# A sparse-mask residual and an attention block on one core: another order of tile projections, row maxima and head outputs around the pairs

## The reference

```python
# step 1: the 10240 largest entries of a scaled outer product get +1 (diagonal excluded)
adj = s * cond * softmax(x) / sqrt(n)            # 1024 x 1024 a batch
x = x + (1.0 at the top_k(adj, 10240), else 0.0)
# step 2: conditioned RMS norm, attention with 16 heads of 64, output projection
xn = rms_norm(x, g_norm) * (1 + scale) + shift   # scale, shift = cond @ W_emb + b_emb
q, k, v = split(xn @ W_qkv); q = rms_norm(q, g_q); k = rms_norm(k, g_k)
o = softmax(q @ k.T / 8) @ v
x = x + o + o @ W_out
```

## Time and profile before

| what | value |
|---|---|
| median of 3 runs | 3984.5 us (3980.17 to 3985.11) |
| the profiled execution, its own time | 3988.51 us |
| its span in the trace | 3986.8 us |
| mean granted TensorE clock | 0.978 |
| busy: PE, DVE, ACT, POOL | 3743.1, 2619.9, 1537.1, 1260.9 us |

### The profile page before, as it was taken

How to read it: one execution, slowest core, us unless ns; L and a number is a source line. 1 busy time by engine, 2 the same in 40 slices (tenths; PEclk the granted TensorE clock), 3 DMA queues, 4 the chain that set the end, 5 groups by cost and what they waited for, 6 DMA issues and landing times.

```text
span 3986.8 us, 44387 instructions
## 1 busy us (share of the span) xinstructions
PE 3743.1 (94%) x16035; PEld 2436.3 (61%) x16035; DVE 2619.9 (66%) x4521; ACT 1537.1 (39%) x2724; POOL 1260.9 (32%) x1880
## 2 busy tenths in 40 slices
PE   5885899999998999999998999999998999999999
PEld 2333676666644766667644667667644667666644
DVE  8996677777787677777787677777787333233321
ACT  1004344444434344444434344444433244444430
POOL 2005433333315433333315433333314433333300
PEclk9997799999999999999999999999999999999999
DMA  4003000001025100000125100000033100000022
GB/s 159 0 5 116 17 22 22 22 22 37 22 91 192 34 22 22 22 22 22 33 96 184 42 22 22 22 22 22 22 107 132 47 22 22 22 22 22 22 81 88
DMA packets 165296, 193.68 MB, mean 49 GB/s; under 512 B 7336, under 2 KB 120032, under 8 KB 164064
## 3 DMA queue, kind: packets, MB, share of 16 engines
q1 hardware_dynamic: 165088, 190.98, 15.0%
HBM read 142.72 MB, written 48.23 MB: 48 GB/s over the span
## 4 chain that ended last, share of the span: by engine, by line
PE 73%; DVE 15%; ACT 4%; POOL 4%; issue 3%; DMA 1%; SPq 0%; DVEq 0%; ACTq 0%; POOLq 0%
PE pax L1209 23%; PE ppv L1278 19%; PE pst L1265 10%; PE pax L1245 7%; PE pst L1190 7%; DVE trash L797 3%; DVE xr L832 3%; DVE mx L985 3%; PE pax L1227 2%; POOL xn L419 2%; PE ppv L1209 2%; PE pax L1253 1%; ACT sA L666 1%; DMA pt<-out_x 1%; PE pst L1083 1%
## 5 line engine op out<-in xcount | busy, mean ns | idle before, releaser
L1209 PE MATMUL pax<-wh,xn 128*128 128x384 f32 x3840 | 1060.5, 347 | 21.9 <-POOL xn L419 21.9
L1278 PE MATMUL ppv<-pt,v 128*65 128x512 f32 x2048 | 990.9, 595 | 1.1 <-issue 1.1
L797 DVE TENSOR_SCALAR_CACHE_REDUCE trash<-keys,state 128x2048 uint8<-128x2048 f32 x384 | 900.1, 2344 | 9.8
L985 DVE TENSOR_REDUCE mx<-pax 128x1 f32<-128x512 f32 x960 | 618.6, 686 | 227.5 <-PE pax L1245 207.0
L1209 PEld LDWEIGHTS pax<-wh,xn 128*128 128x128 f32 x3840 | 704.9, 189 | 35.7 <-issue 35.7
L673 ACT ACTIVATE pt<-pst 128x1024 f32<-128x1024 f32 x512 | 524.0, 1023 | 506.2 <-PE pst L1265 447.9
L1209 PE MATMUL pax<-wl,xn 128*128 128x384 f32 x1920 | 649.1, 338 | 0.0
L971 DVE TENSOR_REDUCE ss<-sq 128x4 f32<-128x256 f32 x256 | 107.2, 419 | 759.8 <-ACT sq L648 759.8
L1245 PE MATMUL pax<-sA 65*128 65x512 f32 x960 | 466.0, 531 | 21.9 <-ACT sA L661 13.0
L1278 PEld LDWEIGHTS ppv<-pt,v 128*65 128x65 f32 x2048 | 278.8, 137 | 298.3 <-issue 224.6
L395 POOL TENSOR_TENSOR wl<-wf,wh 128x1024 fp32r<-128x1024 f32 x96 | 228.7, 2387 | 579.0 <-ACT wh L544 579.0
(11 more groups left out here) (144 smaller groups left out, 4574.6 us busy)
## 6 DMA issues: line engine op xcount, KB each, us to landing
wf<-in_L_cond_W_qkv SPq DMA_DIRECT2D x96, 512.0 KB, 5.4
keys<-in_x SPq DMA_DIRECT2D x32, 512.0 KB, 9.8
xin<-in_x SPq DMA_DIRECT2D x32, 512.0 KB, 4.0
out_x<-xin SPq DMA_DIRECT2D x32, 512.0 KB, 3.2
wo<-in_L_cond_W_out SPq DMA_DIRECT2D x4, 4096.0 KB, 13.5
pt<-out_x SPq DMA_DIRECT2D x64, 256.0 KB, 4.0
out_x<-pt SPq DMA_DIRECT2D x64, 256.0 KB, 2.1
oT_scr<-ostg SPq DMA_DIRECT2D x56, 256.0 KB, 2.0
```

Source lines behind the costliest of these rows:

```text
L797: e.tensor_scalar(trash[:], kv, thr_f, None, ALU.is_ge, ALU.add, accum_out=cnt[:, c:c + 1]).then_inc(z_cnt, 1)
L985: e.tensor_reduce(mx2[:, j // T, j % T, c:c + 1], max_banks(alone, j)[:, c, :], axis=AX, op=ALU.max).then_inc(m_mx, 1)
L1209: i = e.matmul(qkv_bank(alone, t)[:, 0:6 * DH], xn[:, a, k, t * P:(t + 1) * P], w[:, k, :, :].rearrange("p s c -> p (s c)"), start=(k == 0 ...
L1278: i = e.matmul(ppv[0:DH + 1, c, :], v2[:, par, kt, hh, :], pt[:, kt % 2, c * HALF:(c + 1) * HALF], start=(kt == 0), stop=(kt == T - 1))
```

## The change

- **Two units ahead.** `scores` and `exp` of unit t + 2 now stand in unit t, so two score tiles are under way. Tile 0 is projected before unit 0, in two parts of 12 products, tiles 1 and 2 in unit 0, and tile t + 2 in units 1 to 5. `transpose_tile(t + 1)` stands right behind `prep_tile(t + 2)`. DVE's `prep_split` of a tile now stands in the tile's own iteration, between its two counts.
- **Maxima over more products.** The table `slots` gives for each of units 8 to 15 what stands between the two products of `values`, and twice what stands behind the scores. Before, one item stood in each of 18 gaps of units 9 to 15.
- **Both heads turned at the next pair's start.** `out_move` of head 0 goes to `ostg` and that of head 1 to `heads_t`; both `out_tokens` and `normalise` stand at the beginning of the next pair, or of the boundary. `max_row` of head 1 goes through `pst`.
- **Boundary.** SP stores a half before it waits to load the next tile. `add_half` comes earlier among the `finalise_tile`s, `prep_sums(gp, 0)` stands before the last `finalise_tile`, and PE projects one more half ahead of the features and of tile 0 (q = 3 to 7, then 8 with the features, then 9; before, q = 3 to 6, 7 with the features, then 8).
- POOL's `zero_row` waits for the previous pair's last values, not for tile 0.

```diff
+    def row_banks(hh):
+        return pst[:, 2:4, :] if hh else pax
+    def evicted(hh):
+        return heads_t if hh else ostg
...
-                    self.finalise_tile(fb, t)
+                    self.keep_tile(fb, t)
                 if ob is not None:
-                    if t == 1:
-                        self.store_half(ob, 0)
-                    if t > 0:
-                        self.store_half(ob, t)
+                    for q in ([0, 1], [2, 3], [4], [5], [6], [7], [8], [9])[t]:
+                        self.store_half(ob, q)
+                if fb is not None and t + 2 < T:
+                    self.next_tile(fb, t)
...
             if prep:
-                e.wait_ge(a_qkv, T * (gp + 1) + 1)
+                e.wait_ge(t_pv, CST + 2 * T * gp)
...
-        def out_move(self, gp, hh):
+        def out_move(self, gp, hh, stored):
             e, g = self.e, 2 * gp + hh
             e.wait_ge(t_pv, CST + T * (g + 1))
...
+            if hh == 0:
                 e.wait_ge(d_ost, 32 * stored + 16)
+            e.activation(evicted(hh)[0:DH + 1, :], ppv[0:DH + 1, :, :].rearrange("p a b -> p (a b)"),
+                         ACT.Copy).then_inc(t_mv, 1)
...
         def pair(self, b, i, par, search, prep, first):
             e, gp = self.e, PAIRS * b + i
+            z = STEPS * b + 4 * i
+            before = [step_before(b, i, t) if search else None for t in range(T)]
...
             self.exp(gp, 0, 0)
             self.max_row(gp, par, 1)
+            if prep:
+                self.prep_tile(gp + 1, 1 - par, 0, z=before[0])
+            elif search:
+                self.search_tot(before[0])
...
+            self.exp(gp, 0, 1)
+            if not first:
+                self.out_rows(gp - 1, 0)
+            for t in range(2 * T):
+                if t == T - 1:
+                    self.out_move(gp, 0, (PAIRS - 1) * b + i)
+                if prep and t == 0:
+                    self.prep_tile(gp + 1, 1 - par, 1)
+                if prep and t == 1:
+                    self.stack_tile(gp + 1, 1 - par, 1)
+                if prep and t == 12:
+                    self.max_row(gp + 1, 1 - par, 0)
+                if t + 2 < 2 * T:
+                    self.exp(gp, (t + 2) // T, (t + 2) % T)
                 if t == 0 and not first:
...
+                    self.out_rows(gp - 1, 1)
+                if prep and t == 0:
+                    self.stack_tile(gp + 1, 1 - par, 0)
+                    self.prep_tile(gp + 1, 1 - par, 2, z=before[2])
+                if prep and 1 <= t <= T - 3:
+                    self.prep_tile(gp + 1, 1 - par, t + 2, z=before[t + 2])
+                    self.stack_tile(gp + 1, 1 - par, t + 1)
+                if prep and t == T - 1:
+                    self.stack_tile(gp + 1, 1 - par, T - 1)
+                if prep and gp + 2 < PAIRS * B and t in (9, 11, 13):
+                    self.split_w(gp + 2, (t - 9) // 2)
...
             gp = PAIRS * fb
             self.ties(fb, 0)
-            self.ties(fb, 1)
             if ob is not None:
                 self.normalise(PAIRS * ob + PAIRS - 1, 1)
-            self.ties(fb, 2)
-            self.ties(fb, 3)
+            for c in range(1, 4):
+                self.ties(fb, c)
             self.ranks(fb)
             for t in range(T):
+                if t == T - 1 and ob is not None:
+                    self.prep_sums(gp, 0)
                 self.finalise_tile(fb, t)
                 if ob is None and t == 2:
                     self.conditioning()
-                if t == 1:
-                    self.add_half(ob, 0)
-                if t > 0:
-                    self.add_half(ob, t)
-            self.add_half(ob, 8)
-            self.prep_sums(gp, 0)
+                for q in ([0, 1], [2, 3], [4], [5], [6], [7], [8], [])[t]:
+                    self.add_half(ob, q)
+            if ob is None:
+                self.prep_sums(gp, 0)
             self.prep_split(gp, 0)
...
+            if not first:
+                for hh in range(2):
+                    self.normalise(gp - 1, hh)
             for t in range(T):
                 before = step_before(b, i, t) if search else None
                 if prep:
                     self.prep_sums(gp + 1, t)
-                    if t == T - 1:
-                        self.normalise(gp, 0)
-                    if t > 0:
-                        self.prep_split(gp + 1, t - 1)
-                    if before is not None:
-                        self.search_update(before)
-                    if search:
-                        self.search_count(z + t // 2, 2 * (t % 2))
-                    if t == T - 1:
-                        self.prep_split(gp + 1, t)
-                    if search:
-                        self.search_count(z + t // 2, 2 * (t % 2) + 1)
-                else:
-                    if t == T // 2:
-                        self.normalise(gp, 0)
-                    if before is not None:
-                        self.search_update(before)
-                    if search:
-                        self.search_count(z + t // 2, 2 * (t % 2))
-                        self.search_count(z + t // 2, 2 * (t % 2) + 1)
-            if search and not prep:
-                self.search_update(z + 3)
+                if before is not None:
+                    self.search_update(before)
+                if search:
+                    self.search_count(z + t // 2, 2 * (t % 2))
+                if prep:
+                    self.prep_split(gp + 1, t)
+                if search:
+                    self.search_count(z + t // 2, 2 * (t % 2) + 1)
             if prep:
                 for j in range(2 * T):
                     self.row_max(gp + 1, j)
-                self.normalise(gp, 1)
+            else:
+                self.normalise(gp, 0)
+                if search:
+                    self.search_update(z + 3)
...
+                if hh:
+                    e.wait_ge(t_mv, 2 * gp + 1)
+                else:
+                    e.wait_ge(t_on, CST + 2 * gp)
             e.wait_ge(t_ex, CST + w + 1)
...
             e, g = self.e, 2 * gp + hh
-            e.wait_ge(t_mv, g + 1)
+            e.wait_ge(t_mv, 2 * gp + 2)
+            e.wait_ge(t_on, CST + g)
...
         def pair(self, b, i, par, search, prep, first):
             e, gp = self.e, PAIRS * b + i
+            z = STEPS * b + 4 * i
+            before = [step_before(b, i, t) if search else None for t in range(T)]
...
+            slots = {8: [None, None, 0], 9: [1, 2, 3], 10: [4, 5, 6], 11: [7, None, None], 12: ["row", None, 8],
+                     13: [9, 10, 11], 14: [12, 13, 14], 15: [15, None, None]} if prep else {}
             if first and b > 0:
                 e.wait_ge(o_add, 2 * T * b - 2)
             self.scores(gp, par, 0, 0)
             if not first:
+                self.out_tokens(gp - 1, 0)
+            e.wait_ge(m_mx, 4 * T * (gp + 1))
+            if prep:
+                self.prep_tile(gp + 1, 0, hi=4)
+            if not first:
                 self.out_tokens(gp - 1, 1)
-            self.max_row(gp, 1)
+            e.wait_ge(t_ex, CST + 2 * T * gp)
             if first and b > 0:
                 e.wait_ge(o_add, 2 * T * b)
-            for t in range(T):
-                if t < T - 1:
-                    self.scores(gp, par, 0, t + 1)
-                else:
-                    self.scores(gp, par, 1, 0)
-                self.values(gp, par, 0, t)
-                if t == 0:
-                    e.wait_ge(m_ev, 2 * gp + 2)
-                    if not first:
-                        self.out_rows(gp - 1, 0)
-                if prep and t > 1:
-                    if t == 2 and not first:
-                        e.wait_ge(t_oe, 2 * gp)
-                    self.transpose_tile(gp + 1, t - 2)
-                if prep:
-                    self.prep_tile(gp + 1, t, z=step_before(b, i, t) if search else None)
-                elif search and t in (0, 4):
-                    self.search_sum(step_before(b, i, t // 2))
+            self.max_row(gp, 1)
+            if prep:
+                self.prep_tile(gp + 1, 0, z=before[0], lo=4)
+            elif search:
+                self.search_sum(before[0])
+            e.wait_ge(m_ev, 2 * gp + 2)
+            self.scores(gp, par, 0, 1)
+            if not first:
+                self.out_rows(gp - 1, 0)
+            for t in range(2 * T):
+                gap = slots.get(t, [None] * 3)
+                self.values(gp, par, t // T, t % T, lambda: fill(gap[0]))
+                if prep and t == 0:
+                    self.prep_tile(gp + 1, 1)
+                if prep and t == 1:
+                    self.transpose_tile(gp + 1, 1)
+                if t + 2 < 2 * T:
+                    self.scores(gp, par, (t + 2) // T, (t + 2) % T)
                 if t == 0 and not first:
                     self.out_rows(gp - 1, 1)
...
+                    e.wait_ge(t_oe, 2 * gp)
+                if prep and t == 0:
+                    self.transpose_tile(gp + 1, 0)
```

(33 more changed lines are left out.)

133 lines of the change are left out of this document (52 added, 81 removed).

## The result

| | median | runs | profiled span | granted clock |
|---|---|---|---|---|
| before | 3982.34 us | 4, 3978.39 to 3985.11 | 3986.8 us | 0.978 |
| after | 4078.23 us | 4, 4073.52 to 4078.43 | 4076.5 us | 0.977 |

What follows compares the result with a forecast made beforehand. PE was taken to bound the kernel, holding 73% of the chain that ended last. 3988.5 + 100 (pairs) - 14 (boundaries) + 1.5 (fourth last pair) = 4076 profiled, so 4072 us; range 3990 to 4112.

Steps and rivals of the forecast that it cites:

- Bunches: Units 9, 10, 13 and 14: two maxima in direct succession make PE stand 1.1 us each time, 4.4 us a pair.
- The second part: Pair from the first maximum on: contents, changes of kind, bunches and small waits sum to 30.7 us, 3.2 more than before.
- The first part: Pair up to the first maximum: loses 3.3 us, gains new waits, 67.9 us in all, bounds 66 and 69.5.
- tile 0's turning: At a pair's start, `transpose_tile(0)` waits 1.5 us for ACT's second `ostg` copy, which reads the bank it writes.
- two sums: Sums over partitions at even tiles' ends: PE waits 0.2 us for DVE two or three times, 0.5 us a pair.
- DVE's wait for POOL: In odd iterations of the first part, DVE's split waits for POOL's rounding: 1.0 us of idle.
- the rival of a slower POOL chain: POOL's chain, at 4.5 us, sets DVE's pace: 2.5 us more in 21 pairs with a search, 4125 us; chance 0.10.
- The pair: A pair of heads with preparation: 3.6 us more than 94.58, for 28 pairs +100 us.
- Last pair and boundary: Final sum 7 us later, boundary gains; net 4.7 us less each, three times -14; fourth last pair +1.5.
- the bunches cost little: Rival for maxima in succession: DVE is ready ahead of both products, so the kernel takes 3950 us, faster; chance 0.10.
- The boundary that gives more: Rival: DVE's boundary waits all go, each 15 us shorter, pairs cost only 1.5 more: 3982 us, no change; chance 0.07.
- the clock would not matter inside a pair: Granted clock stays 1.00 in a pair despite waits of 1 us; new waits at most 1.5 us, so nothing was priced.

Runs made afterwards that it cites:

- x1_spread: Changed kernel with the second of a unit's three maxima moved ahead of the unit's scores, unit 14's bunch kept: 4011.99 us, ratio 1.0059 to the kernel before.
- x4_before_bunched: Kernel before, with only four pairs of maxima put in direct succession in units 10 to 14: 4104.86 us, ratio 1.0297 to the kernel before.
- x2_rows_first: Changed kernel with `out_rows` and its `ostg` copy ahead of unit 2's scores and `exp`: 4065.46 us, ratio 1.0197 to the kernel before.
- x3_split_late: Changed kernel with DVE's splits of the odd tiles behind both counts of the iteration: 4074.72 us, ratio 1.0221 to the kernel before.
- x9_rows_and_split: Changed kernel with the `ostg` copy ahead of `exp` 2 and odd tiles' splits behind both counts, except tile 7's: 4032.57 us, ratio 1.0106 to the kernel before.
- x7_old_boundary: Changed kernel with the boundary's old order of stores, halves and `prep_sums` under the new pairs: 4103.02 us, ratio 1.0287 to the kernel before.
- x5_pax_row: Changed kernel; last pairs alone send the maxima row through `pax` between both `out_tokens`, sum and first `out_rows` behind unit 0's values: 4063.44 us, ratio 1.0186.

## Why the prediction was right

It gave 4072 us and the median is 4078.23. The main mechanism held. The closeness is in part luck: of the 4076 put for a profiled execution (4078.19 came), the pairs cost 25.5 us less than said and all that lies around them 27.7 more. The 4 us between the profiled execution and the median, which the kernel before had, are not there in the changed one.

- **Bunches.** 1.1 us of standing each, four a pair, was the largest term. By starts they are 1.09, 1.10, 1.10 and 1.09. The second part was put at 30.7 and takes 30.20; its single waits were put at 0.2 each and are 0.22 to 0.26. x1_spread takes 2.35 a pair away by order alone, and x4_before_bunched puts 2.9 into the kernel before by order alone.
- **The first part.** Put at 67.9, it takes 67.41. `out_tokens` waits some 0.3 (0.3 said), tile 0's turning 1.46 (1.5), two sums 0.17 and 0.16 (0.5), and unit 8 shows none. DVE's wait for POOL was put at 1.0 and is 1.1, so the rival of a slower POOL chain did not come. The prediction added the waits of this part one by one. The runs show that it is not a sum: tile 0's wait and the sums' cannot be taken out one at a time (x2_rows_first, x3_split_late and x9_rows_and_split).
- **The pair.** +3.6 was said, +3.03 came with a search and +2.8 without. The first pairs of the batches, priced like the others, cost +0.7: the list of new waits took no account of their having no heads to turn. Together 74.5 us in place of 100 for 28 pairs; about 15 of the difference lie in the steady pairs and 11 in the first.
- **Last pair and boundary.** This is the mis-sized term: -4.7 a boundary was said, -14 in all, and +2.9 a boundary came, last pair and boundary together. By the prediction's own cut, the final sum comes 65.7, 64.4 and 65.4 us behind the last pair's first scores, where the earlier trace rows has 55.17: 10 us later, not 7. From there to the row of the next maxima the three boundaries are 4.5, 5.3 and 11.6 us shorter, 7.1 on average, where 11.7 was said. The order in the boundary does bring what it promised in kind (x7_old_boundary: 19 to 25 us for three, part of it perhaps the clock, and the 3.38 of the earlier trace rows gone). The fourth last pair, put at +1.5, costs 5.6. One part of this was priced at nothing: the dip of the clock at a last pair's start, 6.8 us at 0.50 (3.4 in the second), and so up to 3.4 lost. x5_pax_row, which shortens the waits there, takes some 4.2 from each last pair, the waits included.
- **Rivals.** That the bunches cost little (3950) is excluded by x1_spread. One reading against it was wrong: at 1005.21 in the earlier trace rows not both banks were still being read, since the next j's first product starts there in the first bank; only the second was, until 1005.75, and that one holds the bunch back. The boundary that gives more (3982) had the direction of x7 but neither the size nor the cheap pair. That the clock would not matter inside a pair is right for this kernel's steady pairs (1.00 in the one shown, none at 0.50), and wrong for its last pairs and as a general step, as x4_before_bunched shows.

What stays open: how the 8 us by which the three boundaries of one kernel differ (179.3, 176.6, 171.0) divide. Two things differ in the trace. The third boundary prepares no keys for a further search, and DVE is busy for 112 us in it, against 140 and 138; the old order did not gain by that (180.4 before, 183.1 in x7_old_boundary). And the clock is at 0.50 for 17.1, 11.5 and 9.1 us. No run separates them.

## What to carry to other kernels

Where a producer goes round two banks with one reader, ask of each group how much other work the engine has until it needs the same banks again, and put the groups one to a gap: two in direct succession cost 1.1 us here, though the sum of the work stayed the same. An edit that takes one wait away and gains nothing may be hidden by a second wait on another engine; try the two together before giving either up. When a start or an end of a loop has less work to put between its steps than the middle has (here the last pair without preparation), it needs an order of its own.

## What the hardware did that was not expected

The granted clock fell to 0.50 without a long pause of PE. At a last pair's start PE stood for 1.18 us, ran for some 1.4 and stood for 0.93; the clock fell during this second wait, for 6.8 us. In the four last pairs it fell between the end of the first wait and that of the second. In x4_before_bunched it fell behind waits of 0.42 and 0.3 us in 12 of 28 pairs, for 3.4 or 6.8 us, while the changed kernel, with four bunches and waits of 0.55 a pair, shows no dip in its steady pairs. Which of these a kernel gets was not settled here. The Trainium skill describes such a case (TensorE: Matmul & The Clock Gate, section A second HAM failure mode: psum-queue depth-cycling), for bf16 products of 512 columns: small pauses between groups of products that go round banks can be frequent enough to make the clock swing. The dips of x4_before_bunched agree with it; the changed kernel's clock of 1.00 over a pair shows that bunches alone do not bring them.
